# A graph transformer layer on one core: who splits the output projection's first weights, and who makes six low parts of the first expert

## The reference, cut to what matters

```python
xn = _layernorm(x)                        # x is 1250 x 1024, f32
x = x + gnn(xn, edges, W, b) + mix(xn)    # graph convolution, and linear attention:
    # mix: q, k, v = xn @ Wq.T, Wk.T, Wv.T (+ biases), 16 heads of 64
    #      phi(t) = (exp(t @ orf.T / 64**.25 - norm) + 1e-6) / sqrt(256)
    #      out = phi(q) @ (phi(k).T @ v) / (phi(q) @ sum(phi(k)))
    #      return out @ Wo.T + bo
x = x + moe(_layernorm(x))                # 8 experts of 1024 x 1024, top 2 by gate logits
return x
```

## Time and profile before

| | |
|---|---|
| median of 3 runs | 1501.32 us (1500.39 to 1505.74) |
| the profiled execution | 1501.28 us |
| its span in the trace | 1499.7 us |
| busy, share of the span | PE 91%, PEld (weight loads) 80%, DVE 52%, ACT 37%, POOL 29% |
| granted TensorE clock, mean | 0.963 of full speed |
| attention's last pair, from its features to the first row tile | 980.8 to 1026.15 us |
| chunks 0 and 1 of the projection | 1026.15 to 1154.3 us |
| logits of the last tiles and routing | 1154.3 to 1199.5 us |
| experts | from 1199.5 us |

### The profile page before, as it was taken

How to read it: one execution, slowest core, us unless ns; L and a number is a source line. 1 busy time by engine, 2 the same in 40 slices (tenths; PEclk the granted TensorE clock), 3 DMA queues, 4 the chain that set the end, 5 groups by cost and what they waited for, 6 DMA issues and landing times.

```text
span 1499.7 us, 26473 instructions
## 1 busy us (share of the span) xinstructions
PE 1371.4 (91%) x8203; PEld 1207.1 (80%) x8204; DVE 787.2 (52%) x1608; ACT 562.1 (37%) x957; POOL 428.6 (29%) x429
## 2 busy tenths in 40 slices
PE   5788888999999999999999999979999399999896
PEld 2465665798999999999999999967888387778785
DVE  7855344445455656565565656574454624444541
ACT  7321322221144544445454545441122224333431
POOL 7422424334331111110101010044023423333332
PEclk9999999999999999999999999967999599999998
DMA  4110102245410000000000000013245356766843
GB/s 161 47 29 35 47 35 78 67 132 167 128 48 29 29 25 17 28 17 25 28 14 28 14 28 0 0 56 93 67 157 189 123 175 197 211 208 209 279 130 54
DMA packets 58100, 127.78 MB, mean 85 GB/s; under 512 B 7626, under 2 KB 28826, under 8 KB 58048
## 3 DMA queue, kind: packets, MB, share of 16 engines
q1 hardware_dynamic: 48016, 96.79, 18.8%
q0 software_dynamic: 10032, 30.30, 8.6%
HBM read 91.46 MB, written 37.43 MB: 86 GB/s over the span
## 4 chain that ended last, share of the span: by engine, by line
PE 75%; DVE 8%; issue 6%; ACT 4%; DMA 4%; POOL 1%; DVEq 1%; SPq 1%; POOLq 0%; ACTq 0%
PE PB L1615 7%; PE PB L1711 7%; PE PB L1713 7%; PE PB L1712 7%; PE PB L1749 5%; PE PB L1772 4%; PE PB L1926 4%; PE PB L1927 4%; PE PB L1929 4%; PE PB L1696 3%; PE PB L1698 2%; PE PB L1697 2%; PE PB L1656 2%; PE PB L1684 2%; PE PB L1657 2%
## 5 line engine op out<-in xcount | busy, mean ns | idle before, releaser
L1711 PE MATMUL PB<-xh,hw 128*128 128x416 f32 (+1 forms) x576 | 204.0, 354 | 0.0
L1713 PE MATMUL PB<-xh,hw 128*128 128x416 f32 (+1 forms) x576 | 203.2, 353 | 0.0
L1712 PE MATMUL PB<-xl,hw 128*128 128x416 f32 (+1 forms) x576 | 203.1, 353 | 0.0
L1615 PE MATMUL PB<-ohs,ohd 128*128 x534 | 120.2, 353 | 36.1 <-issue 23.8
L1926 PE MATMUL PB<-mwh,mth 128*128 128x512 f32 x368 | 149.5, 406 | 3.9 <-DVE mwl L1571 3.4
L1927 PE MATMUL PB<-mwl,mth 128*128 128x512 f32 x368 | 145.3, 395 | 0.0
L715 POOL CAST hw<-hraw 128x1024 fp32r<-128x1024 f32 x24 | 25.0, 1040 | 419.3 <-DVE qphi L1314 197.4
L1615 PEld LDWEIGHTS PB<-ohs,ohd 128*128 x534 | 52.2, 98 | 101.6 <-issue 84.1
L1187 DVE TENSOR_SCALAR ohd<-iota,dc 128x128 f16 x178 | 56.9, 319 | 114.4 <-PE PB L1615 100.8
L1929 PE MATMUL PB<-mwh,mtl 128*128 128x512 f32 x368 | 115.2, 395 | 0.0
L1711 PEld LDWEIGHTS PB<-xh,hw 128*128 128x128 f32 x576 | 108.7, 189 | 1.3
(11 more groups left out here) (290 smaller groups left out, 3080.0 us busy)
## 6 DMA issues: line engine op xcount, KB each, us to landing
mraw<-expert_w SPq DMA_DIRECT2D x64, 512.0 KB, 10.5
count_rests<-ATf POOLq DMA_DIRECT2D x9, 640.0 KB, 3.3
xrow<-x SPq DMA_DIRECT2D x40, 128.0 KB, 3.0
y_scratch<-xrow SPq DMA_DIRECT2D x40, 128.0 KB, 1.9
yrow<-y_scratch SPq DMA_DIRECT2D x20, 256.0 KB, 3.0
x2n_half<-xhat SPq DMA_DIRECT2D x20, 256.0 KB, 2.3
out<-x SPq DMA_DIRECT2D x9, 512.0 KB
ATf<-wg SPq DMA_DIRECT2D x32, 128.0 KB, 2.3
```

The costliest lines, as they stand in the source:

```text
L1615: ins = mm(PB[:, 1536 * s + c0:1536 * s + c0 + n], ohd[:, ds(2 * side + p, 1), :].rearrange("p a n -> p (a n)"), ohs[:, ds(2 * side + p, 1 ...
L1711: mm(bank(i, n), hw[:, wi, 0, k, :], xh[:, k, c0:c0 + n], start=(k == 0), stop=False)
L1712: mm(bank(i, n), hw[:, wi, 0, k, :], xl[:, k, c0:c0 + n], start=False, stop=False)
L1713: ins = mm(bank(i, n), hw[:, wi, 1, k, :], xh[:, k, c0:c0 + n], start=False, stop=(k == KT - 1))
```

## The change

It has five parts.

1. POOL's `split_weights(ro, 0)` goes. ACT makes the eight high parts in the last pair (`high_slab`: four after the first head's exponents, four after the second's), and DVE the eight low parts (`low_slab`: two after each `keep_outputs` but the last, the final two after `keep_turned(1)`).
2. The first stationary tile is made early for slabs 0 to 6, whose `attnT` earlier pairs have written: ACT's part behind its last `high_slab`, DVE's behind its last `low_slab`, which is ahead of `keep_turned(2)` and `keep_turned(3)`. After `attention_over` only slab 7 is left. `sth` and `stl` are placed elsewhere in memory, so that they are free by then.
3. Low parts 2 to 7 of the first expert go from POOL to DVE (`first_low`): three between the last two `choose`, three after `gate` is made.
4. SP stores the last three tiles of `x2` after all weight loads and after `store_x2n(TT - 1)`.
5. `logits(t)` waits for the second of ACT's two copies only ahead of slab 4.

```diff
         wl0 = keep("wl0", [P, KT, CW], F32R, pr)
+        sth = keep("sth", [P, 2, KT, P], F32R, pr)
+        stl = keep("stl", [P, 2, KT, P], F32R, pr)
         wh1 = keep("wh1", [P, KT, CW], F32R, pr)
         wl1 = keep("wl1", [P, KT, CW], F32R, pr)
         wh, wl = (wh0, wh1), (wl0, wl1)
-        sth = keep("sth", [P, 2, KT, P], F32R, pr)
-        stl = keep("stl", [P, 2, KT, P], F32R, pr)
...
+            def store_x2(t):
                 n = LAST if t == TT - 1 else P
                 sp.dma_start(out[t * P:t * P + n, :], x2[0:n, t, :]).then_inc(s_out, 16)
...
                     store_x2n(t - 2)
+                    if t < TT - 1:
+                        store_x2(t - 2)
...
             store_x2n(TT - 1)
+            for t in range(TT - 3, TT):
+                store_x2(t)
...
-            split_weights(ro, 0)
             attention_over(pool)
             split_weights(ro, 1)
...
-            for k in range(2, KT):
-                low(k)
...
-                high_tile(r, src, 0, slice(0, P))
+                a.activation(sth[:, 0, KT - 1], src[:, KT - 1, 0:P], ACT.Copy).then_inc(r.high, 1)
                 high_tile(r, src, 1, slice(P, 2 * P))
...
+            def high_slab(k):
+                act.wait_ge(ro.raw[k % 4], ro.before + 16 * (k // 4 + 1))
+                a.activation(wh0[:, k, :], raw[:, k % 4, :], ACT.Copy).then_inc(ro.whigh, 1)
...
                     project(j + 1, 0, 0)
+                else:
+                    for k in range(4):
+                        high_slab(k)
                 for i in range(6):
                     query_exp(j, 1, i)
+                if last:
+                    for k in range(4, KT):
+                        high_slab(k)
+                    a.activation(sth[:, 0, 0:KT - 1], attnT[:, 0:KT - 1, 0:P], ACT.Copy).then_inc(first_high, 1)
...
+            def low_slab(k):
+                dve.wait_ge(ro.whigh, k + 1)
+                v.tensor_tensor(wl0[:, k, :], raw[:, k % 4, :], wh0[:, k, :].bitcast(F32), ALU.subtract).then_inc(ro.wready, 1)
...
                     stack_lows(j + 1, 0)
+                else:
+                    for k in range(2):
+                        low_slab(k)
                 keep_outputs(0, 1)
+                if last:
+                    for k in range(2, 4):
+                        low_slab(k)
...
+                else:
+                    for k in range(4, 6):
+                        low_slab(k)
                 keep_outputs(1, 1)
...
+                else:
+                    for k in range(6, KT):
+                        low_slab(k)
+                    dve.wait_ge(first_high, 1)
+                    v.tensor_tensor(stl[:, 0, 0:KT - 1], attnT[:, 0:KT - 1, 0:P], sth[:, 0, 0:KT - 1].bitcast(F32), ALU.subtract)
                 keep_turned(2)
                 keep_turned(3)
...
-            lows(ro, attnT, 0, 0, slice(0, P))
+            dve.wait_ge(ro.high, 1)
+            v.tensor_tensor(stl[:, 0, KT - 1], attnT[:, KT - 1, 0:P], sth[:, 0, KT - 1].bitcast(F32), ALU.subtract).then_inc(ro.low, 1)
...
+            def first_low(k):
+                dve.wait_ge(mw_high, k + 1)
+                dve.wait_ge(mw_ready, k)
+                v.tensor_tensor(mwl0[:, k, :], mraw[0][:, k, :], mwh0[:, k, :].bitcast(F32),
+                                ALU.subtract).then_inc(mw_ready, 1)
...
                 choose(t)
+                if t == TT - 2:
+                    for k in range(2, 5):
+                        first_low(k)
...
+            for k in range(5, KT):
+                first_low(k)
             experts(dve, expert)
...
             def logits(t):
-                pe.wait_ge(x2t_evac, 2 * t + 2)
...
                 for k in range(KT):
+                    if k % 4 == 0:
+                        pe.wait_ge(x2t_evac, 2 * t + k // 4 + 1)
```

More of the change, by code:

```diff
@@ L340, in gps_layer @@
         ro = Rows("ro", NC)
+        first_high = sem("first_high")
         g_x = [sem(f"g_x{i}") for i in range(RING)]
```

## The result

The changed kernel took **1484.25 us** in the median of 4 runs (1481.76 to 1489.74), the kernel before 1502.95 us beside it (1500.39 to 1505.74): ratio 0.988, 95% interval 0.9845 to 0.9916, so some 18 us faster. The forecast was 1477.4 us in a range of 1473 to 1490 us. The direction and the range held; the forecast itself was 6.9 us too low. The profiled execution took 1485.56 us, with a span of 1484.0 us.

The account below looks back on a forecast made before the run. PE was taken as the bound, with time to gain only where it waits or runs at its lower clock. 16.5 us (7.7 + 9.7 - 0.9) plus 7.4 in routing made 23.9 off 1501.28: 1477.4 us, range 1473 to 1490.

Parts of the forecast that it names:

- Taking POOL out: Last pair: without POOL's contention DVE's last stack and query_eps run faster, so outputs start earlier; gain 7.7 us.
- The clock: Last pair: PE's clock stays at 1.00 while the outputs are made; gain 9.7 us, bounds 0 and 9.7.
- The forecast's condition: Last pair: PE's gap shrinks from 6.5 to about 1 us, and the clock was taken to stay at 1.00.
- rival A: Last pair: PE's clock falls all the same, so the 9.7 us are not gained: 1487.1 us; chance 0.27.
- Low parts and stationary tile: Last pair to first row tile: DVE's unhidden splits cost 2.6 us, early stationary tile gains 1.7; net loss 0.9 us.
- Row tile at 1009.6 us: First row tile after the last pair: begins 16.5 us earlier, at about 1009.6 us.
- Routing: Routing: three slow DVE operations without POOL beside them gain 6.2 us, logits' earlier start 1.2 us; 7.4 us together.
- D: Experts: DVE's three late first_low hold up POOL's gather for the second expert tile, at most 3.7 us: 1481.1; chance 0.03.
- C: Last pair: waits in the ring of raw weight loads make the kernel slower; a 40 us load gives 1509 us; chance 0.03.
- 16.5 us were forecast: Last pair to first row tile: sum of 7.7 and 9.7 us gained less 0.9 us lost.

Follow-up runs that it names:

- e3: Changed kernel plus throw-away GpSimd casts and subtractions in the last pair, which nothing waits for: 1495.31 us, ratio 0.9959 to the kernel before.
- e1: Kernel before with the attention part of the change alone (expert low parts, x2 stores and logits start as before): ratio 0.9901 to the kernel before.
- e6: Kernel before with throw-away matmuls in both PE gaps ahead of the last pair's outputs (28 and 9): ratio 0.996 to the kernel before.
- e7: Changed kernel with only the six expert low parts put back on GpSimd: 1486.71 us, ratio 0.9918.
- e5: Changed kernel as it is, measured and profiled a second time: 1480.36 us, ratio 0.9875 to the kernel before.
- e2: Kernel before with the routing part of the change alone, last pair as it was: ratio 0.9939 to the kernel before.
- e10: Kernel before, unchanged, profiled a second time: 1497.75 us in one run.
- e11: Kernel before with the attention part of the change alone, profiled a second time: 1491.0 us in one run.
- e4: Kernel before with 28 throw-away matmuls in PE's wait for nk in the last pair: ratio 1.0017 to the kernel before.

## Why the prediction was right, and where it was off

- **Taking POOL out: 7.7 us.** Measured 7.7 to 8.0 us, some 0.3 of it the clock's; e3 shows contention as its cause.
- **The clock: 9.7 us. This is the step that failed, in its size.** For the profile of before it was right: 10.1 us by the table (27.98 - 17.89). But of the four profiles with POOL at work and no filler it alone had the clock down all the way; the other three lost 5.4 to 5.7 us, so the mean is 6.7 us. And the changed last pair does not always keep the clock: e1 lost 5.0 us, 1 of 5, so 1.0 us in the mean. About 5.7 us of 9.7 remain, and e6 measured 6.0 for it alone. These are means of four and five executions. The forecast's condition (a short gap keeps the clock) held in 4 of 5, and rival A happened in the fifth, at half its price.
- **Low parts and stationary tile: 0.9 us lost.** 18.47 against e6's 17.89 us: 0.6 lost. A low part took 0.68 us where 0.69 was taken.
- **Row tile at 1009.6 us**, in the time scale of before: 980.81 + 28.04 = 1008.85.
- **Routing: 6.2 + 1.2 us.** Measured 6.3 and 1.1 (e7). In the changed kernel's first profile the sum was only 6.1 us, in e5 and e2 7.6. What differs is that PE's clock fell 3.5 us behind the chunk's end there (1150 us) and 5.6 us or more behind it in the other two, so more of the last transposes and logits ran at 0.50; no run tests this. D did not show: PE waits for nothing over 0.4 us in the 30 us from the first expert matmul on. Nor did C: the only engine that waits for `raw` behind the last pair is POOL, for chunk 1.
- **What was not in the sum.** It was made against one execution, and it happened to lie 0.04 us from the median, which looked like proof that it was typical. It was not. It was lucky in the loop (no fall, 5 to 7 us against those with one) and unlucky in the last pair (4.4 us more than e10), and the two nearly cancelled. A change that removes only the unlucky part then looks worth more than it is. That the result lies in the range is due in part to the range's reach, which goes up to rival A's price; the mechanisms, contention and the clock behind it, were right. In the two profiles side by side the sum is 17.3 + 6.1 gained, 8.8 lost to the loop's falls, 0.9 lost in the chunk and 2.0 gained in the experts: 15.7 us, the difference of the spans. The last two terms cannot be put down to the change: from the first row tile to the chunk's end the eleven profiles with the same first row tile take 127.3 to 128.8 us, and from the first expert matmul to the end all thirteen take 295.6 to 300.9 us, whatever the kernel.
- By terms as now measured: 7.8 + 5.7 - 0.6 + 7.4 = 20.3 us. The stretch from the last key-value matmuls to the row tile gives nearly the same in one number: 42.4 us in the mean of before, e10 and e2, 29.0 in that of after, e5, e7, e11 and e1, so 13.4 us where 16.5 were forecast. The two sets of the whole change gave 18.0 us (12.6 to 23.3) and 18.7 us (13.3 to 24.1). What is left between 20.3 and 18.5 is inside these intervals and stays open; so does what makes the clock fall near 450 us, which no run here tried to change.

## What to carry to other kernels

Before pricing a clock term, take a second profile: a stretch at the lower clock can be the toss of one execution even where the total equals the median. Contention prices (an operation's time alone against its time beside another engine) repeated here to a few tenths of a microsecond and could be summed; clock prices need a mean over executions. And when a gap in front of a stage is closed, look one stage on in every queue, since a load that nobody waited for (here `yrow` behind eight weight loads) can be the next wait.

## What the runs showed of the hardware that was not expected

- PE's clock fell in e1 at 996 us with no idle time over 1.1 us ahead of it, and stayed down while PE was busy for 12.39 of 13 us; the same program kept its clock there in its next profile (e11).
- Once down in the last pair, it stayed down for 13 us (e1), 20 us (e10) or 41 us (before), through work of the same kind. Closing one gap of two (e4) gave nothing in the mean of twelve executions.
- Work on POOL that nobody waits for cost the kernel 12 us (e3), by slowing DVE (casts from 0.37 to 1.35 us, subtractions from 0.58 to 1.54 us) and by the fall of PE's clock behind it.
- Beside POOL's subtractions of 128x1024 a DVE operation over 128x10 took 2.2 us in place of 0.18 (before, e7), about as long as one of those subtractions (2.3 us).
- The same 128x1024 low part takes 1.23 us on DVE and 2.3 us on POOL (13.88 / 6 in e7).
